# A two-layer kernel on one core: the first router in column groups, and its second half spread over the FFN lead and five GRU steps

## What is computed

```python
x = x + _L0_ffn_ref(_L0_cond_ref(x, fside, cond), ...)    # Sinkhorn plan P = u*K*v, then the first FFN
x = x + _L1_ffn_ref(_L1_cond_ref(x, cond, ...), ...)      # GRU over the 32 steps, then attention and experts
```

```python
logits = x2d @ gate_weight.T
scores = sigmoid(logits);  sfc = scores + gate_bias
# two groups of four experts; the group with the higher sum of its best two stays,
# within it the best two experts (ties to the lower index)
topk_w = scores[best two] / (their sum + 1e-20) * 2.5
cw = zeros((T, E)) with topk_w at the two experts
routed = einsum('tei,ehi,te->th', relu(x @ up)**2, down, cw)
```

## Time and profile before

| | us |
|---|---|
| median of 3 runs | 496.75 |
| lowest, highest | 495.52, 497.52 |
| the profiled execution | 495.69 |
| its span in the trace | 494.0 |

### The profile page before, as it was taken

How to read it: one execution, slowest core, us unless ns; L and a number is a source line. 1 busy time by engine, 2 the same in 40 slices (tenths; PEclk the granted TensorE clock), 3 DMA queues, 4 the chain that set the end, 5 groups by cost and what they waited for, 6 DMA issues and landing times. The chain is left out here.

```text
span 494.0 us, 24301 instructions
## 1 busy us (share of the span) xinstructions
PE 473.6 (96%) x9142; PEld 394.7 (80%) x9142; DVE 349.4 (71%) x1268; ACT 324.0 (66%) x808; POOL 234.6 (47%) x579
## 2 busy tenths in 40 slices
PE   8999999999999999999999998889999988999996
PEld 7899999999977545666666677678888877999996
DVE  6888888888878575766658655477998887734443
ACT  5455555555646963656665666577887768987773
POOL 3244444444453001055344554644477775777454
PEclk9999999999999999999999999999999999999999
DMA  5170000000000065143425000022233344555200
GB/s 178 46 258 0 0 0 0 0 0 0 0 2 2 23 155 136 42 83 86 86 47 131 1 1 1 18 69 81 65 119 110 130 134 149 167 162 162 88 30 27
DMA packets 23394, 34.42 MB, mean 70 GB/s; under 512 B 4096, under 2 KB 14341, under 8 KB 23208
## 3 DMA queue, kind: packets, MB, share of 16 engines
q1 hardware_dynamic: 20560, 27.23, 20.4%
q0 software_dynamic: 2784, 6.56, 3.7%
HBM read 23.88 MB, written 8.26 MB: 65 GB/s over the span
## 5 line engine op out<-in xcount | busy, mean ns | idle before, releaser
L206 ACT ACTIVATE den_v<-ps_g,floor 128x128 f32<-128x128 f32 x124 | 45.5, 367 | 39.5 <-PE ps_g L266 32.4
L266 PE MATMUL ps_g<-buf_a,u_pad 128*32 128x128 f32 x1984 | 66.6, 274 | 0.1
L280 PE MATMUL ps_g<-buf_b,v_pad 128*32 128x128 f32 x1984 | 63.8, 275 | 0.2
L266 PEld LDWEIGHTS ps_g<-buf_a,u_pad 128*32 128x32 f32 x1984 | 52.2, 110 | 2.6 <-issue 0.3
L280 PEld LDWEIGHTS ps_g<-buf_b,v_pad 128*32 128x32 f32 x1984 | 50.2, 110 | 1.7 <-DVE v_pad L374 0.5
L374 DVE RECIPROCAL v_pad<-ps_g 128x32 f32<-128x32 f32 x124 | 38.8, 333 | 15.6 <-PE ps_g L272 13.7
L1433 POOL DMA_INDIRECT out<-buf_d,token_i x39 | 38.5, 987 | 23.8 <-DVE buf_c L1948 17.2
L767 PE MATMUL ps_h<-buf_c,up 128*128 128x512 f32 x96 | 49.1, 607 | 0.6 <-DVE buf_c L1046 0.4
L192 POOL TENSOR_SCALAR held_u<-inv_u 128x8 f32<-128x8 f32 x124 | 23.9, 192 | 45.3 <-DVE inv_u L383 45.1
L1657 PE MATMUL ps_ss<-xT,buf_d 128*128 128x128 f32 x312 | 41.4, 276 | 0.0
L1657 PEld LDWEIGHTS ps_ss<-xT,buf_d 128*128 128x128 f32 x312 | 37.9, 192 | 0.4 <-ACT xT L1783 0.2
(11 more groups left out here) (360 smaller groups left out, 1256.1 us busy)
## 6 DMA issues: line engine op xcount, KB each, us to landing
cw_b<-cw_d SPq DMA_DIRECT2D x16, 512.0 KB, 7.7
buf_c<-sorted_x SPq DMA_DIRECT2D x39, 136.0 KB
buf_a<-in_x SPq DMA_DIRECT2D x8, 256.0 KB, 5.2
buf_d<-in_x_nt SPq DMA_DIRECT2D x1, 2048.0 KB, 8.9
state<-buf_a SPq DMA_DIRECT2D x16, 128.0 KB, 2.0
x<-in_w SPq DMA_DIRECT2D x8, 256.0 KB
buf_b<-in_w SPq DMA_DIRECT2D x8, 256.0 KB
sorted_x<-nobody SPq DMA_DIRECT2D x1, 1088.0 KB, 11.1
```

What stands on the lines that cost most here:

```text
L206: fn(den_v[:, h, :], ps_v[h], ACT.Relu, bias=floor[:, h:h + 1]).then_inc(v_den, 1)
L266: last = mm(ps_v[h][32 * j:32 * j + 32, :], u_pad[:, h, j, 32 * i:32 * i + 32], K[:, t * D:(t + 1) * D], start=i == 0, stop=i == TI - 1)
L280: last = mm(ps_u[h][32 * c:32 * c + 32, :], v_pad[:, h, c, 32 * i:32 * i + 32], KT[:, b * N:(b + BG) * N], start=i == 0, stop=i == TI - 1)
```

## The change

The logits of a half are now four matmuls with the gate's weights (padded from 8 to 32 columns) as the stationary operand and a quarter of P moving. Quarter j of the half goes to output partitions 32j to 32j+31, that is to column group j of the array. The sigmoid takes all 512 columns and 128 partitions at once. A 32x32-block transposition on DVE puts tokens on partitions for the ranking, and another one turns the weights back, so that PE's transposes of them and the copies out of PSUM are gone. The turned scores and weights live in `vb`, a buffer of the attention stage; POOL writes the ones that belong there after step 19 and not at the start. POOL clears `cw` at the start.

`weigh` is cut into `rank`, `find`, `mark`, `share` and `hand_over`. The first half is ranked right after the fourth quarter of P; quarters 5 to 8 of P come behind it on DVE. The second half's `rank` and first `find` stand in the lead, the rest in steps 0, 2, 5, 6 and 7, between `kept` and the wait for tanh. SP writes four quarters each with a DMA of its own; the first repeat waits for the first write alone. The last four quarters are written when step 7 has handed them over, ahead of the repeat of the fifth quarter (q = 4). PE's lead order is new, with ups and downs mixed.

At the GRU's end, two statistics and two aggregations stand before the wait for tanh, and ACT normalises rows 28 and 29, DVE rows 30 and 31.

```diff
-        self.gate_w = mem.sb("gate_w0", [P, 8])
+        self.gate_w = mem.sb("gate_w0", [P, 32])
...
-        cw_t = K[0:E, :]
+        turned = setup.vb[:].rearrange("p k b j r e -> p (k b j r e)")
+        cw_t = turned[:, 0:PARTS * W].rearrange("p (k w) -> p k w", w=W)
+        scores_t = turned[:, PARTS * W:2 * PARTS * W].rearrange("p (k w) -> p k w", w=W)
...
+                sp.wait_ge(w_turned, 1)
+                send_weights(0, w_out0)
+                for q in range(1, QS // 2):
+                    send_weights(q, w_out)
+                sp.wait_ge(w_out0, 16)
                 repeat(0)
-                sp.wait_ge(w_first, 4)
-                sp.dma_start(cw_d[:, W:4 * W], cw_t[:, W:4 * W]).then_inc(w_out, 16)
-                sp.wait_ge(w_out, 32)
+                sp.wait_ge(w_out, 48)
                 repeat(1)
                 for q in range(2, QS):
+                    if q == QS // 2:
+                        sp.wait_ge(w_turned, 2)
+                        for late_q in range(QS // 2, QS):
+                            send_weights(late_q, w_out)
+                        sp.wait_ge(w_out, 112)
                     sp.wait_ge(gated, S.last_gate[q - 2])
                     repeat(q)
...
-                def logits(q):
-                    part, first = divmod(q * STEPS, TP)
-                    for k in range(STEPS):
-                        n = q * STEPS + k
-                        last = mm(ps_l[part][:, first + k, :], pt_n[:, n * B:(n + 1) * B], gate_w[:], start=True, stop=True)
+                def logits(part):
+                    pe.wait_ge(pt_ready, (part + 1) * QS // PARTS)
+                    for j in range(QS // PARTS):
+                        q = part * (QS // PARTS) + j
+                        last = mm(ps_l[part][32 * j:32 * j + 32, :], gate_w[:], pt_n[:, q * W:(q + 1) * W], start=True, stop=True)
                     last.then_inc(l_mm, 1)
...
+                def hand_over(part):
+                    c.step(v.reciprocal(top[:], top[:]))
+                    c.step(v.scalar_tensor_tensor(out=cw[:, :, 0:E], in0=cw[:, :, 0:E], scalar=2.5,
+                                                  in1=top[:, :, None].broadcast_to(wide), op0=ALU.mult, op1=ALU.mult))
+                    v.transpose(cw_t[:, part, :], cw[:].rearrange("p n e -> p (n e)")).then_inc(w_turned, 1)
...
+                    if t >= TAIL + 2:
+                        spread(t - 2)
+                    if t == N - 1:
+                        aggregate(TAIL)
+                        aggregate(TAIL + 1)
+                    if t == 0:
+                        mark(0)
+                    if t == 2:
+                        find()
+                    if t == 5:
+                        mark(1)
+                    if t == 6:
+                        share()
+                    if t == 7:
+                        hand_over(1)
                     dve.wait_ge(c_done, t + 1)
```

More of the change, by code:

```diff
@@ L1005, in _ @@
                 normed(TAIL // 2 - 1)
+                act.wait_ge(st.shifted, 1)
+                for n in (TAIL, TAIL + 1):
+                    act.wait_ge(st.b_mm, (n - st.SLOTS) // 2 + 1)
+                    fn(st.xh[:, n % st.SLOTS, :], st.rows[:, n % st.SLOTS, :], ACT.Identity, scale=st.scale[:, n:n + 1],
+                       bias=st.shift[:, n:n + 1]).then_inc(st.level, 1)
                 normed(TAIL // 2)
@@ L1038, in spread, with aggregate, times_u @@
                     v.bn_stats(st.six[:, n, :], st.rows[:, n % st.SLOTS, :]).then_inc(st.stats, 1)
-                times_v(0)
-                for c in range(CHS):
-                    if 1 <= c and c + 1 < CHS:
-                        times_v(c + 1)
+                def aggregate(n):
+                    dve.wait_ge(st.stats, n + 1)
+                    c.step(v.bn_aggr(st.mean_var[:, n - TAIL, :], st.six[:, n, :]))
+                def times_u(c):
                     dve.wait_ge(u_mm, c + 1)
@@ new lines, in mark @@
+                def mark(n):
+                    c.step(v.tensor_reduce(top[:], eq[:], AX.X, ALU.max))
+                    c.step(tt(hot[:, n], eq[:], top[:, :, None].broadcast_to(wide), ALU.is_equal))
+                    if n == 0:
+                        c.step(v.scalar_tensor_tensor(out=biased[:], in0=hot[:, 0], scalar=-1e30, in1=biased[:],
+                                                      op0=ALU.mult, op1=ALU.add))
+                    else:
+                        c.step(tt(hot[:, 0], hot[:, 0], hot[:, 1], ALU.add))
@@ L1086, in weigh, with share @@
+                def share():
+                    c.step(tt(cw[:, :, 0:E], hot[:, 0], scores[:, :, 0:E], ALU.mult))
+                    c.step(v.tensor_reduce(top[:], cw[:, :, 0:E], AX.X, ALU.add))
                     c.step(v.tensor_scalar(top[:], top[:], 1e-20, None, ALU.add))
+                def hand_over(part):
                     c.step(v.reciprocal(top[:], top[:]))
-                    v.scalar_tensor_tensor(out=cw[:, ns, :], in0=cw[:, ns, :], scalar=2.5, in1=top[:, :, None].broadcast_to(wide),
-                                           op0=ALU.mult, op1=ALU.mult).then_inc(weighed, 1)
@@ L1092, in _ @@
                 dve.wait_ge(early.pref, 1)
                 dve.wait_ge(early.gate_in, 32)
-                for part in range(PARTS):
-                    weigh(part)
+                dve.wait_ge(cleared, 1)
+                rank(0)
+                find()
+                mark(0)
+                find()
+                mark(1)
+                share()
+                hand_over(0)
+                times_u(4)
+                for n in range(5, CHS):
+                    times_v(n)
+                    times_u(n)
@@ L1132, in _ @@
                         add(n)
-                def aggregate(n):
-                    dve.wait_ge(st.stats, n + 1)
-                    c.step(v.bn_aggr(st.mean_var[:, n - TAIL, :], st.six[:, n, :]))
-                for n in range(TAIL, N - 2):
-                    aggregate(n)
                 spread(N - 2)
```

161 lines of the change are left out of this document (74 added, 87 removed).

## The result

| | before | after |
|---|---|---|
| median of 4 runs, us | 496.13 | 491.11 |
| lowest, highest | 494.58, 497.52 | 490.64, 492.17 |
| profiled execution | 495.69 | 491.33 |
| its span | 494.0 | 489.6 |

The ratio is 0.9895 with a 95% interval of 0.986 to 0.993, so 5.0 us faster, by more than the 0.5% that can be told here. The forecast was 491.0.

A forecast was written before the change was run, and what follows sets the result against it. PE was taken to bound the lead. Lead -7.4, steps +2.2, GRU's end -0.3 sum to -5.5 us: 490.2 from the profiled 495.69, 491.3 by the median, stated as 491.0, range 489.0 to 494.3.

The forecast's parts named there:

- Logits and transposes of weights: Lead, PE: two logits groups at 0.86 us each save 4.8 us; 32 weight transposes, 3.5 us, go away.
- Rival 2: Lead: columns don't overlap at 512 wide, each logits group takes 3.4 us; 496.1 us, no change; chance 0.06.
- (a): Lead: first logits need four products P; PE waits 0.5 us, and DVE's ranking starts at 153.2.
- (b): Lead: ranking with two block transpositions takes 9.5 us; PE loses 1.0 us before the seventh transposes of u.
- (c) to (e): Lead: ups 4 to 9 at ACT's pace lose 1.1 us, the second sigmoid 0.5, small start gaps 0.4.
- (f): Lead: first repeated weights, issued at 164.3, land about 171.5, just hidden from the gated downs; 2 us of cover.
- Steps: GRU steps 0 to 7: the rest of the second ranking, partly covered by DVE's waits for tanh, loses 2.2 us.
- The fifth quarter's load: Writes and load after step 7 take 10.4 us, first used after 12.7: 2.3 us of cover, put at nothing.
- Rival 5: Step 10: the fifth quarter's load is late, each microsecond costing one; kernel slower, 499 us at 18 us landing; chance 0.03.
- GRU's end: Two normalisations moved from DVE to ACT, statistics and aggregations ahead of waits: 0.3 us won.
- Rival 3: Lead: the two first loads share queues and land some 12 us after issue; about 494 us; chance 0.08.
- rival 4: Steps: added DVE time has no cover and costs 5.1 us instead of 2.2; 493.9 us; chance 0.07.

The follow-up runs named there:

- after again: The changed kernel, unedited, measured a second time: 490.68 us, ratio 0.9896 to the kernel before.
- experiment 1: Changed kernel with the whole second choice of the second half back in the lead, none in the steps: 495.23 us, ratio 0.9969.
- experiment 6: Changed kernel with products P 5 and 6 made in DVE's idle time before the first ranking: 490.84 us in one run.
- experiment 7: Two reorderings of the changed kernel, second half ranked mostly before DVE's wait for the load ends, the second with PE's order evened out: 489.01 and 489.06 us.
- experiment 4: Changed kernel with the second choice's 15 instructions placed anew: 1 in the lead, the rest in steps 0 to 5: 488.10 us, ratio 0.9826.
- hand_later: Changed kernel with the second half's weights handed over in step 8, not 7, so the fifth quarter's load is later: 495.96 us in one run.
- experiment 3: Changed kernel with the second load of weights issued only when all eight P are made: 491.93 us in one run.
- respread again: The same kernel as experiment 4, measured once more: 489.02 us, ratio 0.9869.

## Why the prediction was right, point by point

The mechanism is the one forecast, and most parts came out near their terms. That the totals agree to 0.1 us (491.11 for 491.0) is luck. The forecast lay 5.75 us under the median of three runs of the kernel before (496.75); with a fourth run that is 496.13, and the gain 5.0 us, 5.7 beside after again. Between the profiled executions it is 4.4 for the sum's 5.5: up to the attention 5.6, and the 1.2 behind it that no term had.

- **Logits and transposes of weights.** Right: a group takes 0.99 us (0.86), the overlap is full, and 32 transposes are gone. The sum left out 0.12 us behind and 0.09 ahead of each group. The drain at a change of tiling (the Trainium skill, TensorEngine Tiling (Array Packing), Key Properties), which I weighed at 0.65 us, is at most these 0.4 us for four edges. Rival 2 is out.
- **(a), (b).** Ranking began at 152.89 (153.2), a block transposition takes 0.71 (0.75, between the ends 0.45 and 0.9), and the weights were ready at 162.44 (162.7). The seventh group of transposes of u began at 163.07 (163.7), with a wait of 0.38 where I had said about 1; with ACT's pace ahead of it 0.5 us was lost.
- **(c) to (e).** Ups 4 to 9 took 6.22 us for 5.16, 1.1 us lost as said. The second sigmoid cost less: ups 18 to 20 took 2.78 us for 2.58, 0.2 lost for 0.5. The lead as a whole: 7.7 for 7.4.
- **(f).** Mis-sized: the load took 8.85 us, not about 7.2. The sum took it for one DMA, but it is two, and the second ends it: in the kernel before they took 5.7 and, issued 0.7 us later, 7.6, which makes 8.3. So the gatings ended at 175.2 and the ranking at 179.6 for 178.4; of 2 us of cover 0.52 was left. It still held. That it held by so little is what experiments 1, 6 and 7 show: whatever is added to DVE behind the gatings is on the path, and whatever is taken from PE meets DVE or ACT. What DVE can do before the load lands is free (experiment 7).
- **Steps.** 0.48 in step 0 (0.47), 0.51 in step 2 (0.47), 0.50 in step 5 of which step 6 took back 0.15 net, so 0.35 for both (0.37), 0.69 in step 7 (0.85, though its terms add up to 0.89): 2.0 for 2.2. The lower end was added up wrongly too: step 7 and half of the rest is 1.5, not 1.0. The mechanism, DVE's wait for tanh as the cover and its idle time before `rh` as the place where a loss is taken back, is what experiment 4 used to win the 2 us again.
- **The fifth quarter's load.** The term that failed, though it cost little: 2.3 us of cover. From the end of the transposition (212.05) the load was issued after 3.2 us (2.6) and took 9.7 (7.7), 12.9 us where I had 10.4. The gating was due 12.5 us after (12.7), so it was late by 0.39 us in one execution; in the other it was not late. Both terms were too small, that of the landing above all: 7.7 is the median over single DMAs, and what counts is the second of a pair, 0.6 us behind and 9.0 long (hand_later 8.3, after again 8.5). Rival 5 priced a late load at one for one. Experiment 5 has 5.7 us for 3.5, as the clock falls behind the wait (2.9 of it), so this rival was nearer than its 0.03 said: a load 3.5 us later takes the whole gain.
- **GRU's end.** 0.2 for 0.3. Rival 3 (shared queues, the first load landed after some 12 us) is out by its 8.85 us, though the second load, which nobody waits for here, did take 12.4 (experiment 3), rival 4 by the steps.
- **A reading.** The GRU matmul at 188.6 is the first on x; the first on the state stands at 189.14. The sum hangs on the former alone.
- **Not in the sum:** the stretch after the GRU, up to 1.2 us slower in single executions.

## What to carry to other kernels

When one engine's work in a full stretch is cut, list when each of the others would be done, in the new order: here DVE's chain and the weights' load were 0.5 us behind PE, ACT not much more, and the cut alone, with DVE's order left as it was (experiment 1), was worth 1.3 us of 5. Small operations moved into a pipelined loop are free in those iterations behind which the engine idles before its next output that is waited for, and not where its wait is short: the same operations cost 2 us in one placing and nothing in the other. A wait of PE of several us that another engine's order makes possible is to be priced with the clock behind it, and a load's cover by the last of its DMAs, at its place in the queue, not by the median over all of them.

## What the hardware showed that I had not expected

- The price of a wait on PE is not its length. Behind waits of 4.38 and 3.25 us the granted clock was 0.50, and 1.6 and 2.9 us more were lost. Behind the waits of 0.7 us in the steps of the kernel after it stayed at 1.00.
- The clock fell in a stretch where PE's records show it busy, with matmuls of 8 columns behind short waits: 2.00 of 2.00 us busy at a granted 0.63, then 0.50. The same place without them kept 1.00 in all other profiled executions; with them there is one.
- Four transposes after a stretch of the attention with little PE work ran at full clock in one execution of a program (respread again, granted 1.00) and at half in another (respread, 0.50, 1.06 us instead of 0.60).
- The first load of a quarter's weights took 8.7 to 10.0 us over the kernels, the fifth 9.0 and 9.7. Of two loads issued right behind each other the first took what it takes by itself (8.85 and 8.87 us), and the second paid: its last DMA landed after 12.4 us instead of 8.9.
- Four f32 matmuls of 512 columns in four column groups take 0.87 us together, as long as one on the full array, with 0.12 us behind and 0.09 ahead of a group.
